# Layer 1's messages in two scaled fp16 parts, their scale from squares summed beside the placing, and one wait a chunk for the gathers

## The reference

```python
x = _layernorm(x + L0(x, edge_index, W1, b1, W2, b2))            # hypergraph convolution, twice
x = _layernorm(x + L1(x, edge_attr_64, We1, ..., src, dst))      # the layer the change is about
x = _layernorm(x + L2(x, edge_index, W_key, ...))                # gate = sigmoid(k[dst] + q[src]); gate * v[src]
x = _layernorm(x + L3(x, edge_index))                            # light graph convolution

def L1(nodes, edges, We1, be1, We2, be2, Wn1, bn1, Wn2, bn2, senders, receivers):
    edge_in = concatenate([edges, nodes[receivers], nodes[senders]], axis=-1)
    h = relu(edge_in @ We1 + be1)            # 206250 x 128: the "messages"
    new_edges = h @ We2 + be2
    agg = segment_sum(new_edges, receivers, num_segments=6250)
    h2 = relu(concatenate([agg, nodes], axis=-1) @ Wn1 + bn1)
    return h2 @ Wn2 + bn2
```

## Time and profile before

| what | value |
|---|---|
| median of 3 runs | 4566.49 us |
| profiled execution | 4560.08 us, its span 4558.5 us |
| mean granted TensorE clock | 0.92 of full speed |
| busy: PE, DVE, POOL, ACT | 3684.6, 2888.4, 2574.3, 1600.4 us |
| 900 scatters of features (L930) | 1106.8 us busy, 196.5 to 1943.3 us |
| 864 gathers of sources (L973) | 1007.9 us busy, 1947.3 to 3231.9 us |
| `residual` and `last_part` (L2429, L2436), 319 each | 328.1 and 329.5 us busy |
| 2089 matmuls of `add_up` (L1396) | 416.7 us busy |
| bytes moved | 254 GB/s over the span, up to 418 GB/s in a slice of 114 us |

### The profile page before, as it was taken

The page is one execution under the profiler, slowest core; times in us unless marked ns, Lnnn a source line. Parts: engine busy times, 40 slices in busy tenths (PEclk is TensorE's granted clock), DMA queues, the critical chain, the costliest instruction groups (busy, mean ns, idle before and its releaser), DMA issues.

```text
span 4558.5 us, 127255 instructions
## 1 busy us (share of the span) xinstructions
PE 3684.6 (81%) x48218; PEld 3255.3 (71%) x48218; DVE 2888.4 (63%) x3816; ACT 1600.4 (35%) x2668; POOL 2574.3 (56%) x2291
## 2 busy tenths in 40 slices
PE   0777699998899998378999999999766777777396
PEld 0656588887899997357777777777655767767396
DVE  6999888887111102268888888888545666666502
ACT  0333399997000000223333333333224544444200
POOL 0288866666555656677777777777203444444100
PEclk9776799999999999689999999999888999999798
DMA  5611188888999997568888888888517767767596
GB/s 163 241 30 30 43 305 319 322 324 325 340 387 385 418 416 279 172 210 267 273 273 275 272 271 272 274 260 274 190 38 240 264 231 239 252 235 247 166 407 249
DMA packets 430076, 1159.85 MB, mean 254 GB/s; under 512 B 111175, under 2 KB 250422, under 8 KB 422712
## 3 DMA queue, kind: packets, MB, share of 16 engines
q1 hardware_dynamic: 331478, 919.45, 56.8%
q0 software_dynamic: 66016, 114.12, 8.4%
q10 hardware_dynamic: 32256, 121.34, 6.8%
HBM read 791.79 MB, written 364.93 MB: 254 GB/s over the span
## 4 chain that ended last, share of the span: by engine, by line
DMA 33%; issue 25%; POOL 17%; PE 16%; DVE 5%; POOLq 2%; SPq 1%; ACT 1%; DVEq 0%; ACTq 0%
DMA feat_slot<-SK,sidx_p 19%; DMA arena<-tab_l_src,SK 7%; POOL arena L854 7%; POOL feat_slot L930 5%; PE PS L1271 4%; POOL arena L973 4%; PE PS L1396 3%; PE PS L1376 2%; DMA sidx_p<-SK 2%; PE PS L1370 2%; DMA arena<-feat_slot 2%; DMA hots<-arena 1%; PE PS L1365 1%; PE PS L1342 1%; DMA SK<-in_edge_attr_dram 1%
## 5 line engine op out<-in xcount | busy, mean ns | idle before, releaser
L930 POOL DMA_INDIRECT feat_slot<-SK,sidx_p x900 | 1106.8, 1230 | 557.0 <-DMA feat_slot<-SK,sidx_p 283.6
L973 POOL DMA_INDIRECT arena<-tab_l_src,SK x864 | 1007.9, 1167 | 266.8 <-issue 216.8
L854 POOL TENSOR_TENSOR arena<-arena 128x448 f16<-128x448 f32 x343 | 363.2, 1059 | 660.6 <-ACT arena L1730 660.5
L1271 PE MATMUL PS<-arena 128*128 128x192 bf16 (+1 forms) x7203 | 615.6, 248 | 104.3 <-DVE arena L2183 62.2
L1271 PEld LDWEIGHTS PS<-arena 128*128 128x128 bf16 x7203 | 606.7, 98 | 111.7 <-DVE arena L2183 62.5
L1438 PE MATMUL PS<-arena 128*128 128x128 f16 x4802 | 459.8, 223 | 134.4 <-DVE arena L2364 73.8
L1442 PE MATMUL PS<-arena 128*128 (+1 forms) x4802 | 439.0, 195 | 0.1
L1438 PEld LDWEIGHTS PS<-arena 128*128 128x128 bf16 x4802 | 313.1, 99 | 161.8 <-issue 147.4
L2429 DVE TENSOR_TENSOR arena<-arena 128x896 f32<-128x896 f32 (+1 forms) x319 | 328.1, 1028 | 150.3 <-ACT arena L1770 136.7
L1370 PE MATMUL PS<-arena 128*128 (+1 forms) x4178 | 418.6, 224 | 0.0
L1396 PE MATMUL PS<-arena 128*128 128x384 bf16 x2089 | 416.7, 337 | 2.1 <-DVE arena L2436 2.1
(11 more groups left out here) (274 smaller groups left out, 6546.6 us busy)
## 6 DMA issues: line engine op xcount, KB each, us to landing
arena<-slot_rows SPq DMA_DIRECT2D x343, 448.0 KB, 5.6
arena<-cnt_t SPq DMA_DIRECT2D x147, 896.0 KB
hots<-arena ACTq DMA_DIRECT2D x175, 672.0 KB
arena<-hots SPq DMA_DIRECT2D x175, 672.0 KB, 4.3
arena<-cnt_t SPq DMA_DIRECT2D x147, 672.0 KB
cnt_t<-arena SPq DMA_DIRECT2D x49, 1568.0 KB
cnt_s<-arena SPq DMA_DIRECT2D x49, 1568.0 KB
arena<-cnt_s SPq DMA_DIRECT2D x49, 896.0 KB
```

The source lines that it names most:

```text
L854: pool.tensor_tensor(halves[i][:, n:2 * n], gated[i], halves[i][:, 0:n], ALU.subtract).then_inc(msg_lo, 1)
L930: pool.indirect_dma_start(feat_slot, bass.IndirectOffsetOnAxis(ap=sidx_p[odd][:, n:n + 1].bitcast(u32), axis=0), fwin[h][:, t * D:(t + 1) ...
L973: pool.indirect_dma_start(qgot[n % 3][:, slot_of[t] * P:(slot_of[t] + 1) * P], None, tab_src[4], bass.IndirectOffsetOnAxis(ap=gidx[odd][:, ...
L1271: last = nc.tensor.matmul(PS[:, at:at + w3], ring[u % RING][:, of:of + P], esplit[:, (i * CH + w) * w3:(i * CH + w + 1) * w3], start=u == ...
```

## The change

Messages: the fp32 message becomes two fp16 parts. ACT's ReLU writes the first into `pair_of_halves`; DVE makes the second in one instruction, max(value, 0) minus the first, from PSUM for slots and from `hid` for naturals. `last_part` is gone, and `add_up` streams 256 columns. PE's `meet` now waits for `msg_lo` of the chunk two before, where it waited for `pre_free`.

Scale: ACT loads the 206250 x 64 edge features once more, in 66 pieces of 125 partitions x 1600 numbers into two buffers, and squares and sums each (`add_squares`): one piece after each window of the placing loop (46 pieces), the other 20 after the last window. DVE's `scale_again` takes the largest sum (through a matmul of PE), makes a power of two of it in 11 steps on [128, 1] or [128, 2] and scales `wpq`, `wtwo`, `we1` and `wfold`; then the flag follows.

Gathers: the six semaphores `q_in` become two, one for chunks of even and one for chunks of odd number, and POOL waits once ahead of a chunk's six gathers.

```diff
+FPARTS, FPIECES = 125, 66
+FEDGES = E // FPARTS // FPIECES
...
-        q_in = added[4:7] + [gate_in, gate_out, ft_in]
+        q_in = added[4:6]
...
+                        if not first or n >= 2:
+                            pool.wait_ge(q_in[n % 2], (j * NCH + n - n % 2) * (TN * 8))
                         pool.nop(nofuse=True)
                         for t in range(TN):
                             tile = n * TN + t
-                            if not first or n > 0:
-                                pool.wait_ge(q_in[t], j * (NCH * 16) + n * 16)
-                                pool.nop(nofuse=True)
                             pool.indirect_dma_start(...)\
-                                .then_inc(q_in[t], 16)
+                                .then_inc(q_in[n % 2], 16)
...
                         if kind2 == "slots":
-                            pe.wait_ge(pre_free, slots_at(j2, c2))
+                            pe.wait_ge(msg_lo, count_at(j2, q2))
...
-                    parts = upper[(q + odd) % 2][:, 0:3 * n * H].rearrange("p (s b f) -> p s b f", s=3, b=n)
-                    o = PS[:, bank:bank + 3 * H].rearrange("p (s f) -> p s f", s=3)
+                    parts = pair_of_halves[(q + odd) % 2][:, 0:2 * n * H].rearrange("p (s b f) -> p s b f", s=2, b=n)
+                    o = PS[:, bank:bank + 2 * H].rearrange("p (s f) -> p s f", s=2)
...
+            def load_piece(n):
+
+                of = feat.rearrange("(p n) f -> p (n f)", p=FPARTS)
+                act.dma_start(fpiece[n % 2], of[:, n * FEDGES * D:(n + 1) * FEDGES * D]).then_inc(fpiece_in[n], 16)
+
+            def add_squares(n, odd, m):
+
+                act.wait_ge(fpiece_in[odd], m * 16 + 16)
+                nc.scalar.activation(fpiece[odd], fpiece[odd], ACT.Square, accum_out=fsum[:, bass.ds(n, 1)]).then_inc(fsum_made, 1)
+                if isinstance(n, int) and n + 2 >= FPIECES:
+                    return
+                act.wait_ge(fsum_made, n + 1)
+                of = feat.rearrange("(p n) f -> p (n f)", p=FPARTS)
+                act.dma_start(fpiece[odd], of[:, bass.ds((n + 2) * (FEDGES * D), FEDGES * D)]).then_inc(fpiece_in[odd], 16)
...
                 with act.Fori(0, (NB - 3) // 2) as i:
                     body(i * 2 + 3, 1)
+                    add_squares(i * 2, 0, i)
                     body(i * 2 + 4, 0)
+                    add_squares(i * 2 + 1, 1, i)
                 for w in range(NB, NB + 3):
                     body(w, w % 2, w)
+                for n in range(NB - 3, FPIECES):
+                    add_squares(n, n % 2, n // 2)
...
-                        nc.scalar.activation(hid[i][:, 0:TN * H], hid[i][:, 0:TN * H], ACT.Relu).then_inc(relu_made, 1)
+                        if not isinstance(j, int) or j > 0 or q >= 2:
+                            act.wait_ge(agg_made, count_at(j, q) - 2)
+                        nc.scalar.activation(pair_of_halves[i][:, 0:TN * H], hid[c % 2], ACT.Relu).then_inc(relu_made, 1)
...
+            def scale_again():
+
+                TS = V.tensor_scalar
+                dve.wait_ge(fsum_made, FPIECES)
+                step(V.memset(fmax[:, :], 0.0))
+                V.tensor_reduce(fmax[0:FPARTS, :], fsum, AX.X, ALU.max).then_inc(placed_ready, 1)
+                dve.wait_ge(total_made, 2)
...
-                    V.tensor_tensor(hid[i][:, n:2 * n], hid[i][:, 0:n], upper[i][:, 0:n], ALU.subtract).then_inc(msg_res, 1)
-
-                def last_part(j, odd, q):
...
+                    of = PS[:, i * 1024:i * 1024 + n] if kind == "slots" else hid[c % 2]
+                    V.scalar_tensor_tensor(pair_of_halves[i][:, n:2 * n], of, 0.0, pair_of_halves[i][:, 0:n], ALU.max, ALU.subtract)\
                         .then_inc(msg_lo, 1)
```

More of the change, by code:

```diff
@@ L150, in build @@
         epsc = sb("epsc", [P, 2])
-        wsq = carve(100, 2 * H + 3 * D, parts=D + 1)
-        bound = sb("bound", [P, 3])
-        scale_i = sb("scale_i", [P, 6], i32)
+        wsq = carve(112, 3 * H + 3 * D, parts=D + 1)
+        bound = sb("bound", [P, 4])
+        scale_i = sb("scale_i", [P, 8], i32)
         scale_up = scale_i[:, 0:3].bitcast(f32)
+        again_up = scale_i[:, 6:7].bitcast(f32)
+        again_down = scale_i[:, 7:8].bitcast(f32)
+        fsum = carve(98.5, FPIECES, parts=FPARTS)
+        fpiece = [carve(99 + 6.5 * i, FEDGES * D, parts=FPARTS) for i in range(2)]
+        fmax = sb("fmax", [P, 1])
         scale_down = scale_i[:, 3:6].bitcast(f32)
@@ L272, in build @@
         fnat = [carve(119.5 + 1.5 * i, TN * D) for i in range(3)]
-        hid = [carve(124 + 10.5 * i, 3 * CH * P) for i in range(2)]
+        hid = [carve(124 + 3 * i, TN * P) for i in range(2)]
+        pair_of_halves = [carve(130 + 3.5 * i, 2 * CH * P, f16) for i in range(2)]
         gated = [carve(122.5 + 3.5 * i, CH * D) for i in range(3)]
         halves = [carve(124.25 + 3.5 * i, 2 * CH * D, f16) for i in range(3)]
-        upper = [h.bitcast(bf16).rearrange("p (n two) -> p n two", two=2)[:, :, 1] for h in hid]
         fT_slots = [carve(145 + 2 * i, 4 * P) for i in range(2)]
@@ L386, in build @@
         gate_made = sem("gate_made")
-        msg_res = sem("msg_res")
+        fpiece_in = [sem(f"fpiece_in{i}") for i in range(2)]
+        fsum_made = sem("fsum_made")
         msg_hi = sem("msg_hi")
@@ L1007, in fold_weights @@
                 pe.wait_ge(fold_kept, 1)
-                nc.tensor.matmul(PS[:, 2048:2048 + 2 * H + 3 * D], wnorm[:, 0:1].to_broadcast((D + 1, P)), wsq[:, :],
+                nc.tensor.matmul(PS[:, 2048:2048 + 2 * H + 3 * D], wnorm[:, 0:1].to_broadcast((D + 1, P)), wsq[:, 0:2 * H + 3 * D],
+                                 start=True, stop=True)
+                nc.tensor.matmul(PS[:, 2560:2560 + H], wnorm[0:D, 0:1].to_broadcast((D, P)), wsq[0:D, 2 * H + 3 * D:],
                                  start=True, stop=True).then_inc(fold_made, 1)
@@ L1190, in place_edges @@
                 nc.tensor.matmul(PS[0:1, 0:1], ones_col[:, :], placed1[:, :], start=True, stop=True).then_inc(total_made, 1)
+                pe.wait_ge(placed_ready, 2)
+                nc.tensor.matmul(PS[:, 512:513], ones_col[:, 0:1].to_broadcast((P, P)), fmax[:, :], start=True, stop=True)\
+                    .then_inc(total_made, 1)
             def make_counts():
@@ L1613, in body @@
                         keep_slots(w - 2)
+                act.wait_ge(fold_made, 1)
+                for i in range(2):
+                    load_piece(i)
                 act.wait_ge(natT_made, 1)
@@ L2410, in add_sources @@
                     dve.wait_ge(pre_made, count_at(j, q))
-                    if not isinstance(j, int) or j > 0 or q >= 2:
-                        dve.wait_ge(agg_made, count_at(j, q) - 2)
-                    for t in range(TN):
-                        dve.wait_ge(q_in[t], j * (NCH * 16) + (c + 1) * 16)
+                    dve.wait_ge(q_in[c % 2], (j * NCH + c - c % 2 + 2) * (TN * 8))
                     n = TN * H // 2
-                    V.tensor_tensor(hid[i][:, 0:TN * H].rearrange("p (k n) -> p k n", k=2),
+                    V.tensor_tensor(hid[c % 2].rearrange("p (k n) -> p k n", k=2),
                                     PS[:, i * 1024:(i + 1) * 1024].rearrange("p (k n) -> p k n", k=2)[:, :, 0:n],
@@ L2428, in residual @@
                         dve.wait_ge(relu_made, naturals_at(j, c))
-                    V.tensor_tensor(hid[i][:, n:2 * n], hid[i][:, 0:n], upper[i][:, 0:n], ALU.subtract).then_inc(msg_res, 1)
-                def last_part(j, odd, q):
-                    i = (q + odd) % 2
-                    n = (CH if place(j, q)[0] == "slots" else TN) * H
-                    dve.wait_ge(msg_res, count_at(j, q))
-                    V.tensor_tensor(hid[i][:, 2 * n:3 * n], hid[i][:, n:2 * n], upper[i][:, n:2 * n], ALU.subtract)\
+                    of = PS[:, i * 1024:i * 1024 + n] if kind == "slots" else hid[c % 2]
+                    V.scalar_tensor_tensor(pair_of_halves[i][:, n:2 * n], of, 0.0, pair_of_halves[i][:, 0:n], ALU.max, ALU.subtract)\
                         .then_inc(msg_lo, 1)
@@ L2468, in body @@
                         select_sums(j, q)
-                        if old and place(old[0], old[2])[0] == "slots":
-                            last_part(*old)
                         if q == 3 and not first:
```

35 lines of the change are left out of this document (25 added, 10 removed).

## The result

The changed kernel takes 4594.23 us (median of 8 runs, 4582.71 to 4613.45) against 4562.9 (8 runs, 4552.73 to 4585.29) on the same chip: a ratio of 1.0062, 95% interval 1.0042 to 1.0083. It is 31 us slower; the forecast was 4520, 43 us faster than that. The profiled execution is the slowest of the eight (4613.45 us, span 4611.9), 53.4 us above the span of before. Four differences make up these 53.4 us.

| stretch | before | after | difference | forecast |
|---|---|---|---|---|
| first gather | 1947.3 | 2026.6 | +79.3 | +69 |
| first to last gather | 1284.6 | 1239.8 | -44.8 | -115 |
| tail of slot chunks | 70.9 | 69.0 | -1.9 | 0 |
| end of layer 1 to end | 1255.7 | 1276.6 | +20.9 | 0 |

A forecast was written before the change was run, and what follows sets the result against it. POOL's gathers were taken to bound layer 1's pass. Gathers starting later, +69, and a shorter pass, -115, gave -46 against the profiled 4560.1: 4514, or 4520 as a median; whole range 4452 to 4606 us.

The forecast's parts named there:

- the 115: Layer 1's pass: us saved by gathers that DVE's instructions delay less, 4.8 us a pair, 53.7 to 48.9.
- The 48.7: Layer 1's pass: us PE alone needs for a pair of 7 slot and 6 natural chunks before the change.
- Rival 2: Layer 1's pass meets the DMA engines; slot chunks' ring (load, compare, store, load) limits gain to 24: 4611 us; chance 0.13.
- A gather's price: Layer 1's pass: DVE instructions with two SBUF inputs or bf16 delay POOL's gathers, 0.94 us at shortest, 1.170 on average.
- rival 3: Layer 1's pass: the max-and-subtract from PSUM still holds POOL; gain 71, time 4565 us; chance 0.12.
- Squares behind the loop: After the last placing window: 20 pieces over 5 engines, 6.9 us each, delay the counts' start by 126 us.
- rival 1: Squares behind the placing loop: pieces use all 16 engines, gathers start +8, time 4459 us; chance 0.15.
- Squares in the loop: Placing loop: 46 pieces squared in ACT's idle time cost 0; up to 2 us x 46 = 92 without cover.
- Rival 4: Placing itself slows, ACT's cover lost or one engine carrying the pieces: 4560 to 4610 us or far beyond; chance 0.08.
- The cost in the end: Start of layer 1's gathers: the counts' delay of 126 moves it from 1947.3 to 2016, +69 us (55 to 95).
- the absorbed 57 us: Ahead of layer 1's gathers: POOL's feature writes need 57 us more than the tables, which swallows that much delay.
- Waits once per chunk: POOL's gathers in layer 1's pass: fewer waits worth 0; 260 us, cut to 228, if the gap went to nothing.

The follow-up runs named there:

- the kernel before with both reliefs: Kernel before the change, with PE's pass written out and slot features asked for ahead of the stored selections: 4579.3 us, ratio 1.0024.
- features first: Changed kernel with PE's pass written out, plus slot features asked for right after a chunk's slot rows, on their own semaphores: 4547.98 us, ratio 0.996.

## Why the prediction was wrong

The time came inside the range, but the kernel got slower where it was forecast to get faster. Point by point:

- *The step that failed:* "PE's pair is 48.7 - 4.5 = 44.2. PE stays below POOL's 48.9, so this adds nothing to the 115; it is what lets PE follow." The 48.7 were put together from one natural and one slot chunk without a stall, and the waits were taken as spare time. What was left out stood in the trace: PE's ten idle times of "issue" (31.6 us in all, up to 4.5) and the feature waits. They cost at most 9 us of the pass while POOL took 53.6 us a pair, as the kernel before with both reliefs shows, and became the bound as soon as POOL was faster. A pair came to 51.6 us: of the 7.4 above 44.2, the stalls are 2.4 and the feature waits 3.6; the other 1.4 were not taken apart, but PE's granted clock in the pass fell from 0.97 to 0.94. The pass gave 45 us, not 115. With the loop written out it gave 69, with features first 98. Rival 2 had the right ring and the right sign. It put the lengthening on busy DMA engines. The slot features did take longer to land, 5.6 us at the median instead of 4.7, but the order of SP's issues is what made PE wait for them, and the rival did not know of the loop's stall. "It decides from a gain below 69" was the right point.
- *A gather's price* was right in mechanism and nearly in size: 1.014 us for 1.03 to 1.05. A subtraction that reads PSUM did not hold POOL (0.944 us under it, 0.945 under nothing): rival 3 is out.
- *Squares behind the loop*: +136.7 for +126, by five engines as argued; rival 1 is out. The step lacked 5.6 us: the first two pieces are asked for beside the index windows, and the class matching starts at 116.5 instead of 110.9 (with the pieces asked for later, the last window ended as in the kernel before). Most of the other 5 us is the first transfer behind the last window: its square began 13.5 us after the one before it, where 8.9 (6.9, and 2 for the stores beside it) were allowed. The next 17 came 7.0 us apart, where 6.9 was assumed.
- *Squares in the loop*: 0, as said. Rival 4 is out.
- *The cost in the end*: +79.3 for +69; the absorbed 57 us were as read. What the step did not see is that these 57 us also covered a stage that takes 35 us more in some executions.
- *Waits once per chunk*: "Worth 0" was right in the changed kernel. Where POOL sets the pass they cost 13 to 19 us.
- *Tail*: unchanged, as said.

In sum -46 became +32.6: 70 from the pass and 10 from the start of the gathers, less 2 in the tail.

## What to carry to other kernels

When the engine that sets a stage is to become faster, price the second engine from a whole period of its loop, its jump back and its waits included, not from its densest stretch; idle times that cost nothing today are the next bound. Slack ahead of a stage is not only room for a delay: it also covers stages that vary from one execution to the next, and whoever uses it up pays for those too. A transfer's row count decides how many engines carry it: 125 rows went over 5, and cut into 112 and 13 they went over 16 and 13, which brought a piece from 7.0 to 3.8 us.

## What the runs showed of the hardware that was not expected

- PE stood 5.2 to 6.2 us each time its stream went back to the start of a loop of two pairs (some 1100 matmuls); 2.1 to 4.5 in the kernel before. In each stall of the changed kernel one packet of 16384 bytes starts on the profile's instruction queue. Written out, the same stream had no such stall in the whole pass.
- Stages of small products ran at 1.2 or at 2.4 GHz from one execution to the next, 93 to 96 or 128 to 131 us for the same work. From the end of layer 1 to the end it was 1251 to 1256 us in six profiles, 1275 to 1280 in six and 1294 in one.
- One wait a chunk gave POOL six stalls of up to 7.2 us in a pass, put down to nothing, ahead of the same six gathers in eight kernels.
- In the kernel before a gather that began under no DVE instruction took 0.945 us on average, and under `add_sources`, with one input in PSUM, 0.958. Under the fp32 `residual` of a slots chunk (two SBUF inputs) it took 1.226, and under the bf16 `select_rows` of one 1.219.
